# Attention probabilities turned to key rows by DMA transposes, with four score buffers and a third PSUM bank for scores, in a decoder layer on one core

## The reference, cut to what matters

```python
scores = jnp.einsum('blhd,bmhd->bhlm', q, k) * scale
scores = jnp.where(mask[None, None], scores, -1e+30)      # causal
attn = jax.nn.softmax(scores, axis=-1)
out = jnp.einsum('bhlm,bmhd->blhd', attn, v)
return out.reshape(B, L, H * DV) @ w_o
```

## Time and profile before

| what | us |
|---|---|
| median of 3 runs (1407.82 to 1408.37) | 1408.01 |
| profiled execution, first to last instruction | 1403.7 |
| TensorE busy | 1112.1 |
| VectorE busy | 1103.2 |
| ScalarE busy | 703.6 |
| GpSimd busy | 237.7 |

### The profile page before, as it was taken

The page is one execution under the profiler, slowest core; times in us unless marked ns, Lnnn a source line. Parts: engine busy times, 40 slices in busy tenths (PEclk is TensorE's granted clock), DMA queues, the critical chain, the costliest instruction groups (busy, mean ns, idle before and its releaser), DMA issues.

```text
span 1403.7 us, 29983 instructions
## 1 busy us (share of the span) xinstructions
PE 1112.1 (79%) x8718; PEld 706.9 (50%) x8740; DVE 1103.2 (79%) x2984; ACT 703.6 (50%) x1481; POOL 237.7 (17%) x475
## 2 busy tenths in 40 slices
PE   1535688899999999999999999999863644446998
PEld 1323455666656665666666666666431323223554
DVE  5689598888788788887887877778459788886886
ACT  1549366665565565655555555555312430533443
POOL 1100121211111121112112111111003222222111
PEclk9759899999999999999999999999985766678999
DMA  9100000000000010000010000010451100000001
GB/s 361 40 0 0 8 1 9 9 2 9 8 0 7 32 36 7 7 0 7 0 67 0 0 2 1 5 55 1 151 170 40 60 31 0 0 0 0 38 37 46
DMA packets 27316, 43.81 MB, mean 31 GB/s; under 512 B 1528, under 2 KB 12792, under 8 KB 26752
## 3 DMA queue, kind: packets, MB, share of 16 engines
q1 hardware_dynamic: 27264, 43.15, 8.8%
HBM read 35.80 MB, written 7.34 MB: 31 GB/s over the span
## 4 chain that ended last, share of the span: by engine, by line
PE 50%; issue 23%; DVE 15%; POOL 6%; ACT 4%; DMA 1%; ACTq 0%; DVEq 0%; SPq 0%; POOLq 0%
PE bank L1760 10%; PE bank L1699 7%; PE bank L1745 5%; PE bank L1732 4%; PE bank L1633 4%; PE bank L1665 3%; PE bank L1721 2%; PE bank L1717 2%; PE bank L1718 2%; PE bank L1720 2%; PE bank L1719 2%; POOL arena L412 2%; DVE arena L1414 1%; DVE arena L1429 1%; DVE scal L1518 1%
## 5 line engine op out<-in xcount | busy, mean ns | idle before, releaser
L1141 ACT ACTIVATE arena<-bank,arena,scal 128x128 f32<-128x128 f32 (+3 forms) x256 | 158.3, 618 | 203.2 <-POOL arena L998 202.2
L1154 ACT ACTIVATE arena<-bank 128x256 f16<-128x256 f16 (+3 forms) x256 | 179.3, 700 | 112.9 <-PE bank L1732 112.5
L1760 PE MATMUL bank<-arena 128*128 (+1 forms) x768 | 180.4, 379 | 11.8 <-issue 5.7
L1414 DVE TENSOR_REDUCE arena<-bank 128x1 f32<-128x128 f32 (+3 forms) x256 | 124.8, 488 | 72.0 <-PE bank L1722 70.6
L998 POOL TENSOR_TENSOR arena<-arena,scal 128x1 f32<-128x1 f32 x256 | 53.2, 208 | 626.9 <-DVE arena L1414 626.9
L1431 DVE SCALAR_TENSOR_TENSOR arena<-arena 128x128 f16<-128x128 f32 (+3 forms) x256 | 141.1, 551 | 9.1
L1429 DVE TENSOR_SCALAR arena<-arena 128x128 f16<-128x128 f32 (+3 forms) x256 | 125.9, 492 | 14.0 <-DVE arena L1423 0.3
L1699 PE MATMUL bank<-arena 128*128 (+1 forms) x576 | 136.4, 382 | 0.5 <-DVE arena L1462 0.5
L1732 PE MATMUL bank<-ident,arena 128*128 128x128 f16 x1280 | 113.4, 219 | 24.4 <-DVE arena L1431 18.5
L1745 PE MATMUL bank<-arena 128*128 128x512 f16 (+3 forms) x768 | 116.4, 302 | 6.1 <-issue 3.7
L1760 PEld LDWEIGHTS bank<-arena 128*128 (+1 forms) x768 | 72.4, 97 | 89.9 <-issue 25.0
(11 more groups left out here) (216 smaller groups left out, 2254.4 us busy)
## 6 DMA issues: line engine op xcount, KB each, us to landing
arena<-in_L_attn_w_qb SPq DMA_DIRECT2D x1, 4608.0 KB, 23.4
arena<-in_x SPq DMA_DIRECT2D x4, 1024.0 KB, 5.2
arena<-in_L_attn_w_o SPq DMA_DIRECT2D x1, 4096.0 KB, 33.8
arena<-in_fside_BxS2xS SPq DMA_DIRECT2D x4, 1024.0 KB, 5.3
arena<-in_L_ffn_w SPq DMA_DIRECT2D x8, 512.0 KB, 10.4
out<-arena SPq DMA_DIRECT2D x16, 256.0 KB, 2.0
arena<-in_x SPq DMA_DIRECT2D x12, 256.0 KB, 2.7
x_after_attention<-arena SPq DMA_DIRECT2D x3, 1024.0 KB, 4.4
```

What stands on the lines that cost most here:

```text
L1141: act.activation(PF[:, (g % 2) * L:(g % 2) * L + n], banks[S_BANKS[g % 2]][:, 0:n], ACT.Exp, bias=NB[:, g % 2:g % 2 + 1], scale=sc_exp, ac ...
L1154: act.activation(dst[:, :, 0:k + 1, k * P:(k + 1) * P], src[:, :, 0:k + 1, :], ACT.Copy).then_inc(pt_te, 1)
L1414: dve.tensor_reduce(NEGM[:, g % 2:g % 2 + 1], banks[S_BANKS[g % 2]][:, 0:n], AX.X, ALU.max, negate=True).then_inc(s_max, 1)
L1760: last = pe.matmul(banks[Y_BANK][:, :], ot(gp, a, k, (q & 3) * P, P), wo(b, gp * GH + k), start=(k == 0 and n == 0), stop=(k == GH - 1 and ...
```

## The change

`probs_t` on TensorE and `pt_evac` on ScalarE go. In their place SyncE's `turn_probs` issues one DMA transpose for each step, from `PH` straight to `PT`, once the low half is written; for the first tile of a head it also waits until the values of two heads before are done. `PH` now holds high and low half block by block, so one transfer takes both, and `PT` is ordered to match. `PF` and `PH` have one place for each k (four in all) in place of two. `exps` waits for the low half of four steps before; the high half waits for the transpose of the same k one head before; `values` waits for the four transposes of its head, each with its own semaphore. VectorE makes the row scale right after the row maximum, before the other work of the step. The bank that held the turned blocks becomes the third bank for scores, and `scores` waits for the exp of three steps before. SyncE's loop is written out in full, and the token loads, stores and reloads stand at fixed steps between the transposes; the first 3 MB of weights of the next stage are issued after the transpose of step 3 of the last pair. The same in words for what is cut: `row_scale` is the first half of `normalise`, `NEGM`, `NB`, `SUM`, `RC` and `R4` have four places, and `first_weights` holds the wait and the four loads that stood at the head of `later_sync`.

```diff
@@ buffers @@
-        PF = take(2 * L)
-        PH = take(2 * 2 * L, fp16)
+        PF = take(10 * P)
+        PH = take(20 * P, fp16)
...
-        small = take(32)
-        NEGM, NB, SUM, RC = (small[:, 2 * k:2 * k + 2] for k in range(4))
-        R4 = small[:, 8:10]
+        small = take(40)
+        NEGM, NB, SUM, RC, R4 = (small[:, 20 + 4 * k:24 + 4 * k] for k in range(5))
...
+        pt_in = [sem(f"pt_in{k}") for k in range(TB)]
...
-        S_BANKS, T_BANK, O_BANK, Y_BANK, Q_BANK, R_BANK, P_BANK = (0, 1), 2, 3, 4, 5, 6, 7
+        S_BANKS, T_BANK, O_BANK, Y_BANK, Q_BANK, R_BANK, P_BANK = (0, 1, 2), 2, 3, 4, 5, 6, 7
...
         def pt(hp, hl, kt, q, n):
-            o = ((hp * 2 + hl) * TB + kt) * L + q
+            o = ((hp * TB + kt) * 2 + hl) * L + q
...
+        def pt_blocks(hp, k):
+
+            return PT[:, hp * 4096:(hp + 1) * 4096].rearrange("p (t q) -> p t q", t=2 * TB)[
+                :, 0:2 * (k + 1), k * P:(k + 1) * P]
+
+        def pf(k):
+            return PF[:, k * (k + 1) // 2 * P:(k + 1) * (k + 2) // 2 * P]
+
+        def ph(k):
+            return PH[:, k * (k + 1) * P:(k + 1) * (k + 2) * P]
+
+        def ph_part(k, hl):
+
+            return ph(k).rearrange("p (t l c) -> p t l c", l=2, c=P)[:, :, hl, :]
@@ SyncE @@
-                sp.wait_ge(xa_out, 16 * b + 16)
-
-            for d in range(4):
-                load_xt(TB + d)
-            with sp.Fori(1, 3) as b:
-                load_xt(4 * b + 4)
-                load_xt(4 * b + 5)
-                load_xt(4 * b + 6)
-                store_xa(b - 1)
+
+            def reload_xa(b):
+                sp.wait_ge(xa_out, 16 * b)
                 load_xa(b)
-                load_xt(4 * b + 7)
-            store_xa(2)
-            load_xa(3)
+
+            def turn_probs(i, g):
+
+                Hd, k = 2 * i + (g >> 2), g & 3
+                sp.wait_ge(s_lo, 8 * i + g + 1)
+                if k == 0 and Hd >= 2:
+                    sp.wait_ge(pv_mm, Hd - 1)
+                sp.dma_start_transpose(pt_blocks(g >> 2, k), ph(k)).then_inc(pt_in[k], 16)
+
+            load_xt(TB)
+            for i in range(NPAIR):
+                for g in range(8):
+                    turn_probs(i, g)
+                    if g == 3 and i % 2 == 0 and i // 2 + 5 < NT:
+                        load_xt(i // 2 + 5)
+                    if i % 8 == 4 and i >= 12:
+                        if g == 3:
+                            store_xa(i // 8 - 1)
+                        if g == 7:
+                            reload_xa(i // 8)
+                    if i == NPAIR - 1 and g == 3:
+                        first_weights(sp)
             later_sync(sp)
@@ ScalarE @@
-                if not (isinstance(G, int) and G < 2):
-                    act.wait_ge(s_lo, G - 1)
...
-            def pt_evac(i, g):
...
-                act.activation(dst[:, :, 0:k + 1, k * P:(k + 1) * P], src[:, :, 0:k + 1, :],
-                               ACT.Copy).then_inc(pt_te, 1)
+                if not (isinstance(G, int) and G < 4):
+                    act.wait_ge(s_lo, G - 3)
+                act.activation(pf(k), banks[S_BANKS[g % 3]][:, 0:n], ACT.Exp, bias=NB[:, k:k + 1], scale=sc_exp,
+                               accum_out=SUM[:, k:k + 1]).then_inc(s_exp, 1)
@@ VectorE @@
-            def normalise(G, g):
+            def row_scale(G, g):
...
+            def probs_hi(i, g):
+
+                k, G = g & 3, 8 * i + g
                 dve.wait_ge(s_r4, G + 1)
-                if not (isinstance(G, int) and G < 2):
-                    dve.wait_ge(pt_t, G - 1)
...
+                if not (isinstance(i, int) and i == 0 and g < 4):
+                    dve.wait_ge(pt_in[k], 16 * (2 * i + (g >> 2)))
+                dve.tensor_scalar(ph_part(k, 0), pf(k).rearrange("p (t c) -> p t c", c=P), R4[:, k:k + 1], None,
+                                  ALU.mult).then_inc(s_hi, 1)
+
+            def probs_lo(G, g):
+
+                k = g & 3
                 dve.wait_ge(s_hi, G + 1)
...
+                dve.scalar_tensor_tensor(out=ph_part(k, 1), in0=pf(k).rearrange("p (t c) -> p t c", c=P),
+                                         scalar=R4[:, k:k + 1], in1=ph_part(k, 0), op0=ALU.mult,
                                          op1=ALU.subtract).then_inc(s_lo, 1)
...
                     row_max(G + g, g)
+                    if g > 0:
+                        row_scale(G + g - 1, g - 1)
+                    elif not first:
+                        row_scale(G - 1, 7)
...
                     if g > 0:
-                        normalise(G + g - 1, g - 1)
+                        probs_hi(i, g - 1)
+                        probs_lo(G + g - 1, g - 1)
@@ TensorE @@
-                if not (isinstance(i, int) and i == 0 and g < 2):
-                    pe.wait_ge(s_exp, 8 * i + g - 1)
+                if not (isinstance(i, int) and i == 0 and g < 3):
+                    pe.wait_ge(s_exp, 8 * i + (g - 2 if g >= 3 else (-1, 0, -2)[g]))
...
-            def probs_t(i, g):
...
-                for hl in range(2):
-                    for kt in range(k + 1):
-                        o = (g % 2) * 1024 + hl * L + kt * P
-                        last = pe.transpose(bank16[T_BANK][:, (hl * 4 + kt) * P:(hl * 4 + kt + 1) * P], PH[:, o:o + P],
-                                            ident16[:, :])
-                last.then_inc(pt_t, 1)
-
             def values(i, h):
 
                 Hd, bp = 2 * i + h, (i >> 3) & 1
-                pe.wait_ge(pt_te, 4 * Hd + 4)
+                for k in range(TB):
+                    pe.wait_ge(pt_in[k], 16 * Hd + 16)
```

More of the change, by code:

```diff
@@ L170, in decoder_layer @@
         srq_pow = sem("srq_pow")
-        s_mm, s_max, s_bias, s_exp, s_rc, s_hi, s_lo, pt_t, pt_te = (
-            sem(n) for n in ("s_mm", "s_max", "s_bias", "s_exp", "s_rc", "s_hi", "s_lo", "pt_t", "pt_te"))
+        s_mm, s_max, s_bias, s_exp, s_rc, s_hi, s_lo = (
+            sem(n) for n in ("s_mm", "s_max", "s_bias", "s_exp", "s_rc", "s_hi", "s_lo"))
+        pt_in = [sem(f"pt_in{k}") for k in range(TB)]
         s_r4 = sem("s_r4")
@@ L359, in xall, with load_weights, first_weights @@
             return at(XALL, n * D, D)
-        def later_sync(sp):
-            def load_weights(u, l, b, after=None):
-                w, s, done = ((fside, WF, wf_in), (ctxw, WC, wc_in))[l]
-                if after is not None:
-                    sp.wait_ge(w_q, after * TB + TB)
-                    sp.wait_ge(done, 32)
-                sp.dma_start(s[u].rearrange("p (t n) -> p t n", t=TB),
-                             w[b].rearrange("(t p) n -> p t n", p=P)).then_inc(done, 16)
+        def load_weights(sp, u, l, b, after=None):
+            w, s, done = ((fside, WF, wf_in), (ctxw, WC, wc_in))[l]
+            if after is not None:
+                sp.wait_ge(w_q, after * TB + TB)
+                sp.wait_ge(done, 32)
+            sp.dma_start(s[u].rearrange("p (t n) -> p t n", t=TB),
+                         w[b].rearrange("(t p) n -> p t n", p=P)).then_inc(done, 16)
+        def first_weights(sp):
             sp.wait_ge(qn_mm, 2 * NPAIR)
@@ L1197, in pair @@
                             prep_cn(*prep)
-                    if g >= 2:
-                        pt_evac(i, g - 2)
-                    elif not first:
-                        pt_evac(i - 1, g + 6)
                     if g == 4 and not last:
@@ L1557, in _ @@
             walk(dve, pair)
-            normalise(8 * NPAIR - 1, 7)
+            row_scale(8 * NPAIR - 1, 7)
+            probs_hi(NPAIR - 1, 7)
+            probs_lo(8 * NPAIR - 1, 7)
             out_lo(2 * NPAIR - 2, 1, GH - 2)
@@ L1706, in scores @@
                 h, k, bp = g >> 2, g & 3, (i >> 3) & 1
-                n, bank = (k + 1) * P, banks[S_BANKS[g % 2]]
+                n, bank = (k + 1) * P, banks[S_BANKS[g % 3]]
                 if k == 0:
@@ L1795, in pair @@
                             project(i - back, heads, prep if j == 0 else None)
-                    if g >= 2:
-                        probs_t(i, g - 2)
-                    elif not first:
-                        probs_t(i - 1, g + 6)
             prep_t(0, T_BANK)
@@ L1821, in _ @@
             walk(pe, pair)
-            for g in (6, 7):
-                probs_t(NPAIR - 1, g)
             values(NPAIR - 1, 1)
```

38 lines of the change are left out of this document (10 added, 28 removed).

## The result

The changed kernel takes 1381.4 us (median of 4, 1380.0 to 1382.7) against 1407.9 for the kernel before: ratio 0.982 [0.981, 0.983]. That is faster by 26.5 us where 53 were forecast. The profiled span went from 1403.7 to 1379.2 us.

A forecast was written before the change was run, and what follows sets the result against it. TensorE was taken to bound the middle and end of the walk, neither engine alone the beginning. Gains of 35 us middle, 17 late, 7 early, less 6 at the end, took 53 off 1408.0: 1355 us, range 1325 to 1440.

The forecast's parts named there:

- TensorE gives up 4.5 us a double pair, at 56 ns a block: In the walk, 40 turning blocks a pair leave TensorE: 2.2 us a pair, 4.5 a double pair.
- the late part: Late in the walk, 801 to 1000 us: double pair to 46.0 us, a gain of 4.2, in all 17.
- The sum of the middle: 287 to 801 us: 47.1 busy, 2.9 idle, 0.7 for the tie make 50.7 for 54.4, in all 35 us gained.
- Early: 158 to 287 us: double pair 46.7 us in place of 49.2, a gain of 2.5, in all 7 us.
- VectorE keeps all its work: VectorE does the same work, its high half in blocks at the kept doubled rate; 44.5 us busy, floor 47.1.
- Rival 2: VectorE becomes the bound by the lost rate of the high half: 29 us gained, 1379 us; chance 0.13.
- The transfer: A DMA transpose of 8 blocks, 256 KB, takes 4.1 us; SyncE's issue takes 15 us a pair and keeps up.
- The room of `values`: Time from low half done to `values` of head 0, less the turning: 5.4 us for the transpose; head 1 has 8.4.
- Rivals 3, 4 and 5: Transfer outlasts its room (0.16); transposes run one after another, 2226 us (0.07); TensorE waits at `values` instead, 1408 us (0.04).
- rival 3: Transfer outlasts the room of `values`: each us beyond costs 32 us; 1480 us at 9 us latency; chance 0.16.
- The end: After the last pair, transposes queue behind 3 MB of weights: `values` 3 to 4 us later, a loss of 6.
- The third bank brings nothing in the middle: Scores run one step further ahead: nothing gained where TensorE bounds, something early.

The follow-up runs named there:

- b1: The kernel before with 16 of the 20 turning blocks of a head left out from the second pair on; 1380.6 us, ratio 0.981.
- b2: The kernel before with TensorE's walk over the pairs written out, without the hardware loop; 1394.1 us, ratio 0.992.
- e1: The changed kernel with `out_hi` put at the end of step 4 of ScalarE, ahead of `rope_hi` and the exp; 1375.1 us, ratio 0.977.
- b3: The kernel before with the walk written out on all four computing engines; 1391.7 us, ratio 0.989.
- e2: The changed kernel with the 384-column high half written as 2 x 3 x 64 elements in place of 3 x 128; 1378.2 us, ratio 0.978.
- b4: The kernel before, written out on all four engines, with 16 of 20 turning blocks a head left out from the second pair on; 1357.7 us, ratio 0.963.
- e4: The changed kernel with each DMA transpose issued twice, the other one into a spare tile; 1435.5 us, ratio 1.021.
- e7: The changed kernel with the first 3 MB of the next stage's weights asked for after the last transposes; 1376.6 us, ratio 0.978.
- e10: The changed kernel with two banks for scores in place of three, scores waiting for the exp of two steps before; 1387.2 us, ratio 0.986.
- e3: The changed kernel with GpSimd's rope sum moved to VectorE; 1377.2 us, ratio 0.979.
- e8: The changed kernel with TensorE's walk over the pairs written out, the other three engines keeping their loop; 1373.5 us, ratio 0.976.

## Why the prediction came out as it did

- *TensorE gives up 4.5 us a double pair, at 56 ns a block.* Right: 51.5 to 47.3 us busy. That the late part then gains 4.2 a double pair: right in number (15.7 of 17 us). It is less sure that TensorE's matmuls alone bound it: b1, which spares them four fifths of the turning, gains 9.5 there, and b2, which spares only register work, 9.3.
- *The sum of the middle.* This step failed. It kept TensorE's 2.9 us of idle time and added 0.7, my choice, for two engines at one floor. The idle time became 5.5, so the gain was 1.6 instead of 3.7: 14.5 for 33 us. I took the idle time for a property of TensorE, and the floor of VectorE for the only other one. But there was a third floor, in the hand-offs between the engines with register work in them. It lay at 52.9 us, 1.5 below the old double pair, whatever did the turning (b1), and it came down when the register work was taken out of TensorE (52.0), of VectorE (51.6), and of all four engines (50.5). Which hand-offs make the round is shown in part only: I take it to be scores, maximum, exp, low half, `out_hi`, `out_lo`, `project`; e1 took the wait for `out_hi` out of it and gained 0.8 us of the double pair. One link showed before: `out_lo` waited 24.9 us for `out_hi`, which I expected to shrink with the freed ScalarE. After, the same wait is 32.5 us:

```profile
DVE arena L1457 <- ACT arena L1178: 32.5, 30, 1.3
```

  ScalarE's copies were not what made it long. And "issue" was 23% of the chain before, which I did not price. With it gone from all engines the middle is 462.9 us for the change, against 486.5 for the kernel before. The 50.5 us at full clock come close to the forecast 50.7, but by two effects of which the forecast had one: from b3's 52.8 the change itself takes 2.2 to 2.3 us a double pair, still not 3.7. In the 50.5 us TensorE is idle for 3.9, where the sum had 3.6.
- *Early.* The price was chosen between VectorE's floor and the old time (2.5 a double pair), and is 0.2 or less. b1 has 129.8 us there too: leaving out most of the turning gained nothing. The clock had a share that the sum did not have: it was at 0.50 for 18.4 us of this part after and for 8.0 before (0.90 for 0.97 in the rows of a double pair). One even pair, with 6.8 us of it in place of 3.4, took 29.69 us for 28.44, which took back what two odd pairs had gained (20.1 for 20.7 each); an even pair without it took 28.45 for 28.44. TensorE's waits after in that part name ScalarE's rope halves and VectorE's preparation; none of the runs separated them, so what holds 49 us there stays open.
- *VectorE keeps all its work.* Right in sum (44.45 for 44.51 us busy). The rate was neither kept nor lost: at three blocks alone it is lost, 187 ns a piece, and e2 shows that it is hardly worth anything in time. Rival 2 had the right size (1379) for the wrong reason.
- *The transfer.* 4.1 us taken for 8 blocks, 3.1 measured (2.3 for 2 blocks, 2.8 at the median of all); SyncE's 15 us a pair are 9.6 (8 x 1.2). The room of `values`, 5.4 us by the sum, is 5.8 to 7.1 in the steady middle. No wait came of the transfer there, and b1, b4 and e4 agree. Rivals 3, 4 and 5 fall, and with them the upper half of my range. For head 1 rival 3 counted half of what exceeds its 8.4 us (0.3 of 0.6, 1.0 of 2.0), without a reason.
- *The end.* 6 us priced; the tail is 3.2 longer, and e7 gives back 3.8. The parts were off and made up for each other: `values` begins 6.4 us later behind the last low half (8.5 for 2.2), not 3 to 4, and less followed from it.
- *The third bank brings nothing in the middle.* Right: with two banks no pair at full clock is longer, and the 6 us of e10 lie in pairs behind a lower clock. That it brings something early is not shown either.

In all, 28 us of the profiled gain are missing (53 forecast, 24.5 measured): 20 in the middle (35 for its 9.4 double pairs), 7 early, 1 late and 3 at the start, less 3 by which the end lost less than priced.

## What to carry to other kernels

Before you credit an engine's saved work in full, leave the work out and time that: one such run of the kernel before gives the floor that the rest has, which no busy share shows. Idle time of an engine is not a constant that survives the change; ask of each wait whether the released instruction began when its releaser ended, or some tenths of a microsecond later with register work in between. Where a loop with addresses in registers feeds short instructions on several engines, try it written out before moving work between the engines: here this was worth 23 to 25 us, about as much as the change itself. And before two variants are compared by their totals, look at the granted clock inside their repeated unit: three variants here gained 0.8 to 0.9 us a double pair at full clock and lost it again in a few microseconds at half clock (e1, e3, e8).

## What the runs showed of the hardware

- Register instructions that stand behind a wait are not done ahead: after `out_hi` ended at 601.41 us, six of them took until 602.07, and the other three `out_lo` of that double pair have six each before them too.
- Address work slows matmuls of 128 columns in a row from 56 to 63 ns each (e8 against after).
- The granted clock of TensorE can fall to 0.50 for a few microseconds inside a walk whose page shows 9 tenths: twelve matmuls of `project` then take 4.42 us in place of 2.76 (e1). It was busy for 0.62 of the 2.60 us before that in e1, and for 0.07 of 2.50 in e8.
- A DMA transpose of fp16 blocks of 128x128 within the core lands in 2.3 us for 2 blocks, 2.5 for 4, 2.8 for 6 and 3.1 for 8 (medians): 0.79 us more for 192 KB more, which as a rate is some 250 GB/s, an estimate. Behind the 3 MB of weights it took up to 9.4. Its issue holds SyncE about 1.2:

```profile
961.28 1.23 SPq L984 DMA_TRANSPOSE arena<-arena  x1
```

  Issued twice as often it still landed in 2.7. The Trainium skill, "VectorE: DVE Perf Modes", section "The three transpose paths", has 1309 ns for one block by the crossbar; taken as a rate, 8 blocks would be 10.5 us, an estimate. The trace does not agree: 8 blocks land in 3.1 us. The same page of the Trainium skill, section "Rules for kernel authors", advises TensorE where PSUM will do. In this kernel the change to the DMA path, with the buffers that belong to it, is the faster (1381.4 us against 1407.9).
- VectorE's doubled rate for a scaling in pieces fell away for three pieces (607 ns at 384 columns) and held for two and four (344 ns at 256, 482 at 512); in 2 x 3 pieces of 64 it held again (415 ns).
